# Cross-attention and mixture-of-experts layer: router logits from the first norm, a second list ahead, a new last expert, new slots

## The reference

```python
f   = layernorm(x)
h   = tanh(ctx @ Ws + f @ W + b)              # for every (token, context row)
rho = h @ w, masked;  att = softmax(rho)
t   = att @ ctx
x   = x + tanh(t . Wcw + bcw) * f + tanh(t . Wcb + bcb)   # two numbers per token
y   = layernorm(x)
probs = softmax(y @ gate)                     # 8 experts
# each expert takes the 512 tokens with its highest probabilities
out = x + gelu(y @ Ws1 + bs1) @ Ws2 + bs2
for e in experts: out[tokens_e] += probs * (gelu(y[tokens_e] @ W1[e] + b1[e]) @ W2[e] + b2[e])
```

## Time and profile before

| | |
|---|---|
| three executions | 950.3, 953.3, 953.63 us (median 953.3) |
| profiled execution, its own time | 951.22 us |
| its span, first to last instruction | 949.5 us |
| mean granted TensorE clock | 0.973 of full speed |
| busy TensorE, ScalarE, VectorE, GpSimd | 814.7, 768.4, 723.5, 200.5 us |
| DMA traffic | 41.84 MB |

### The profile page before, as it was taken

One profiled execution on the slowest core, in us unless ns is written; L12 is line 12 of the kernel. 1 busy time (PEld: TensorE's weight loads), 2 busy tenths in 40 slices (PEclk: granted clock), 3 DMA queues, 4 the chain that ended last, 5 costly groups with the idle time before them and its releaser, 6 DMA issues.

```text
span 949.5 us, 14380 instructions
## 1 busy us (share of the span) xinstructions
PE 814.7 (86%) x5519; PEld 477.7 (50%) x5519; DVE 723.5 (76%) x1482; ACT 768.4 (81%) x601; POOL 200.5 (21%) x434
## 2 busy tenths in 40 slices
PE   6855776668999988999988899987998799999993
PEld 4311221124454443545434454545877688898883
DVE  6898898989877789887698976958864667666530
ACT  4999999999999999999799979965624466766751
POOL 2110220050230041211006000220000154444522
PEclk9999999999999999999999899997999899999997
DMA  8000000010001002000000100013121335555422
GB/s 263 5 0 1 1 1 1 1 43 3 1 2 45 1 21 69 1 1 23 1 1 23 45 1 20 4 31 125 45 73 39 112 89 134 134 133 130 94 23 23
DMA packets 32408, 41.84 MB, mean 44 GB/s; under 512 B 2365, under 2 KB 29011, under 8 KB 32339
## 3 DMA queue, kind: packets, MB, share of 16 engines
q1 hardware_dynamic: 26083, 32.49, 10.4%
q0 software_dynamic: 6144, 8.39, 5.4%
q10 hardware_dynamic: 112, 0.04, 0.0%
HBM read 28.33 MB, written 12.58 MB: 43 GB/s over the span
## 4 chain that ended last, share of the span: by engine, by line
PE 52%; ACT 22%; DVE 16%; issue 6%; POOL 3%; DMA 0%; ACTq 0%; DVEq 0%; POOLq 0%
ACT z L916 18%; PE bank L725 12%; PE bank L850 9%; PE bank L873 9%; PE bank L783 8%; DVE z L1239 7%; PE bank L768 6%; PE bank L701 2%; ACT z L912 2%; PE bank L654 1%; DVE xn L1160 1%; POOL out_dram L1145 1%; ACT u L956 1%; DVE onehot L1527 1%; PE bank L779 1%
## 5 line engine op out<-in xcount | busy, mean ns | idle before, releaser
L916 ACT ACTIVATE z<-z 128x4096 f32<-128x4096 f32 (+5 forms) x157 | 510.3, 3289 | 7.4 <-DVE z L1239 7.3
L1239 DVE TENSOR_SCALAR z<-feat,txt_bias 128x1024 f32<-128x1024 f32 (+1 forms) x704 | 406.5, 649 | 24.9 <-PE bank L725 24.6
L725 PE MATMUL bank<-z,window 128*32 128x512 f32 x2464 | 309.3, 607 | 77.8 <-ACT z L916 75.7
L725 PEld LDWEIGHTS bank<-z,window 128*32 128x32 f32 x2464 | 69.4, 110 | 268.3 <-issue 136.4
L783 PE MATMUL bank<-ws_sb,u 128*128 128x256 f32 x512 | 130.5, 397 | 4.8 <-ACT u L956 4.8
L783 PEld LDWEIGHTS bank<-ws_sb,u 128*128 128x128 f32 x512 | 95.0, 194 | 43.6 <-issue 23.3
L768 PE MATMUL bank<-tr,ws_s 128*128 128x512 f32 x384 | 110.6, 424 | 0.0
L850 PE MATMUL bank<-xg_s,w_s 128*128 128x512 f32 x384 | 101.2, 400 | 3.4 <-DVE xg_s L1553 3.4
L1559 DVE TENSOR_TENSOR hid_s<-hid,hid_s 128x512 fp32r<-128x512 f32 x64 | 44.2, 691 | 76.5 <-ACT hid_s L996 76.5
L873 PE MATMUL bank<-w_s,hid_s 128*128 128x256 f32 x768 | 102.5, 283 | 0.0
L873 PEld LDWEIGHTS bank<-w_s,hid_s 128*128 128x128 f32 x768 | 99.6, 190 | 5.5
(11 more groups left out here) (227 smaller groups left out, 671.4 us busy)
## 6 DMA issues: line engine op xcount, KB each, us to landing
w_raw<-in_L_ffn_W_dram SPq DMA_DIRECT2D x16, 1024.0 KB, 5.5
x_ring<-in_x_dram SPq DMA_DIRECT2D x8, 512.0 KB, 8.1
xn_dram<-xn SPq DMA_DIRECT2D x8, 512.0 KB, 2.9
out_dram<-x_ring SPq DMA_DIRECT2D x8, 512.0 KB, 3.0
u<-in_L_ffn_Ws_dram SPq DMA_DIRECT2D x1, 1024.0 KB, 11.3
ws_sb<-in_L_ffn_Ws_dram SPq DMA_DIRECT2D x1, 1024.0 KB, 13.8
xg<-xn_dram,idx POOLq DMA_INDIRECT x32, 4.1
out_dram<-y,idx POOLq DMA_INDIRECT x32, 3.9
```

What stands on the lines that cost most here:

```text
L725: ins = e.matmul(sums[v][32 * r:32 * r + 32, :], window[:, c, 31 - k:63 - k], z[:, n % ZB, at_piece:at_piece + TOK], start=(v, r) not in b ...
L916: e.activation(part, part, ACT.Tanh).then_inc(signal(*step), 1)
L1239: ins = e.tensor_scalar(z[:, n % ZB, i * width:(i + 1) * width], feat_of(units, c), bias_of(units, t, c), None, ALU.add)
```

## The change

1. **Logits.** `logits` becomes a part of `pre`: TensorE multiplies the turned first norm `tr_x` (stationary, tokens as output rows) with the gate (8 columns), 8 matmuls per unit. `x_spread` (GpSimd) keeps the root of the variance; `logits_out` (VectorE) multiplies by it; `logits_shift` multiplies by the second scale and shifts by the maximum, right after `y_scale`. `gate_cols`, `lg_t` and `logits_turn` go.
2. **Slots.** New tables, `SPLITS` in place of `EARLY_PAIR` and `LATE_SPLIT`; the tail of unit 0 hangs on the end of unit 0, no longer on the start of the next batch; each unit's FFN has its own start and step, with `up` one slot earlier.
3. **Chain.** `router` of unit 6 moves forward; norm, turn and store of unit 7 stand behind `probs_out`; `y_hi` (ScalarE) makes the high part of its turn, `split_hi` of expert 0's weights goes into the tests.
4. **Lists.** List 1 is made before expert 0, with filler between; expert 0 has the beside-steps of every other expert. `EXPERT_FILL` may put filler into expert 0. Experts sum in the banks `RHO` (even) and `DOWN` (odd).
5. **Last expert.** All its ups come first; then token tile by token tile all downs (`e_tile`), `e_out`, and the tile's scatter. The high and low parts of its last four slices go to `last_s`, in the place of the first weights.

```diff
-EARLY_PAIR, LATE_SPLIT = 8, 8
+SPLITS = ((10, 20), (0, 20), (0, 20), (0, 7))
-PRE_EARLY = (20, 21, 22, 23, 24, 24, 25, 26, 26)
-PRE_LATE = (27, 28, 30, 31, 32, 32, 33, 34, 34)
-TAIL_EARLY = (-1, 0, 1, 3, 4, 5, 6, 7, 9, 9, 10, 11, 12, 11, 12, 13)
-TAIL_LATE = (-1, 1, 2, 3, 6, 7, 8, 9, 12, 14, 15, 16, 17, 16, 17, 18)
-TAIL_SINGLE = (-1, 0, 1, 2, 3, 4, 5, 6, 8, 8, 9, 10, 10, 10, 11, 11)
-FFN = (15, 2.2)
-FFN_LAST = (14, 1.7)
+PRE_FIRST = (0, 0, 1, 2, 2, 3, 3, 3, 4, 6, 6)
+PRE_EARLY = (20, 20, 21, 22, 22, 23, 25, 25, 27, 29, 30)
+PRE_LATE = (27, 28, 30, 31, 32, 32, 32, 34, 34, 35, 38)
+TAIL_EARLY = (-1, 0, 1, 3, 3, 4, 5, 8, 9, 10, 10, 11, 13, 13)
+TAIL_FIRST = (-1, 0, 1, 3, 3, 5, 6, 7, 9, 9, 9, 10, 12, 12)
+TAIL_LATE = (-1, 1, 2, 3, 6, 7, 9, 9, 12, 13, 16, 16, 18, 18)
+TAIL_SINGLE = (-1, 0, 1, 2, 3, 5, 6, 10, 8, 9, 9, 9, 12, 11)
+FFN_PLACES = (-1, 1, 2)
+FFN = ((12, 2.0), (33, 2.3), (14, 2.2), (36, 2.2), (14, 1.7), (26, 1.6))
-TAIL_FILL = (2, 4, 0, 0)
-READY_FILL = (1, 0)
-TEST_FILL = (1, 2, 2, 2, 3, 3, 2, 2, 2, 3)
-RANK_FILL = (0, 1, 2, 3)
-LIST_FILL = (2, 1, 0, 1)
+TAIL_FILL = (3, 0, 2)
+READY_FILL = (0, 1)
+TEST_FILL = (2, 3, 2, 3, 2, 1, 1, 2, 3, 1)
+RANK_FILL = (1, 1, 4, 1)
+EXPERT_FILL = (4, 0, 3)
+SECOND_FILL = (7, 5, 1)
+LIST_FILL = (2, 1, 0, 2)
...
-        at_slots(base, TAIL_EARLY, tail(early))
+        at_slots(ends_at[early] + 1, TAIL_EARLY if early else TAIL_FIRST, tail(early))
...
+    n = 0
+    for v, (begin, step) in enumerate(FFN):
+        for m in range(M):
+            n = max(n, starts[v // UPB + 1] + begin + int(step * m))
+            at_slots(n, FFN_PLACES, [[("up", v, m, 0, passes)], [("gelu", v, m)], [("down", v, m, 0, J)]])
+        at_slots(n, (FFN_PLACES[-1] + 1,), [down_ends(v)])
...
-    order += [*end[0], *end[1], ("load_w1", 0), ("load_w2", 0), *end[2], ("att_exp", vb), ("logits_exp", va)]
+    order += [*end[0], *end[1], ("load_w1", 0), ("load_w2", 0), *end[2], ("att_exp", vb), ("logits_exp", va), ("router", va)]
     fill_chain(TAIL_FILL[0])
-    order += [*end[4], *end[5], *end[6], *end[7]]
+    order += [*end[4], *end[5], *end[6], *held, ("exp_again",)]
+    held.clear()
     fill_chain(TAIL_FILL[1])
-    order += [("exp_again",), *end[8], *end[9], *first_split, *ended]
+    order += [*end[7], *end[8], *ended, ("logits_exp", vb), ("router", vb), ("values", NT - 2 * J, NT)]
     fill(TAIL_FILL[2])
-    order += [*end[10], *end[11], *end[13], ("router", va)]
-    fill(TAIL_FILL[3])
-    order += [*end[14], *end[15], ("logits_exp", vb), ("router", vb), ("values", NT - 2 * J, NT)]
+    order += held
     for hf in range(NH):
         order += [("probs_turn", hf), ("probs_out", hf)]
     order += [("load_w1", 1), ("load_w2", 1)]
+    order += [*end[9], *end[10]]
     fill(READY_FILL[0])
...
+    beside = [end[11], end[12], *beside]
+    by_scalar = [[("y_hi", vb, c) for c in range(C)], *[[step] for step in first_split]]
     for k in range(TESTS):
-        order += [("count", k), ("sign_count", k), ("total", k), *held]
+        order += [("count", k), ("sign_count", k), ("total", k), *held, *(by_scalar.pop(0) if by_scalar else [])]
         fill_test(TEST_FILL[k])
         order += [*([("low_digits",)] if k == 0 else beside.pop(0) if beside else []), ("decide", k), ("ask", k)]
...
-    order += [("listed", 0), ("fold", 0), ("folded", 0), ("gather", 0), ("mark", 1), ("mark_slots", 1, 0), ("mark_slots", 1, 1)]
+    order += [("listed", 0), ("fold", 0), ("folded", 0), ("gather", 0)]
+    fill(SECOND_FILL[0])
+    order += [("mark", 1), *(("mark_slots", 1, q) for q in range(4))]
+    fill(SECOND_FILL[1])
+    order += [*(("list", 1, q) for q in range(4)), ("listed", 1)]
+    fill(SECOND_FILL[2])
+    order += [("fold", 1), ("folded", 1), ("gather", 1)]
...
-        if ex == 0:
-            if m < 3:
-                steps += listing(1, *((2,), (3, "list"), ("fold",))[m])
-            elif m < 7:
-                steps += listing(2, *(("mark", 0), (1, 2), (3, "list"), ("fold",))[m - 3])
-        elif m < 6:
+        if m < 6:
             steps += listing(ex + 2, *(("mark",), (0,), (1,), (2, 3), ("list",), ("fold",))[m])
...
+    for m in range(LAG, M):
+        order += up(E - 1, m)
+    for a in range(A):
+        order += [("e_tile", a), ("e_out", E - 1, a)]
+    order.append(("scatter", E - 1))
...
                 elif kind == "logits":
                     v, = args
...
+                    e.wait_ge(*done("x_turned", v, 0))
+                    e.wait_ge(*done("x_turned" if v else "x_turned_first", v, C - 1))
+                    e.wait_ge(loaded["gate"], 16)
                     dst = take(MISC[0])
-                    for c in range(C):
-                        for i in (1, 0):
-                            for j in range(J):
-                                ins = e.matmul(dst[32 * j:32 * j + 32, 0:P], gate_cols[:, c, :],
-                                               tr[:, v % 2, i, c, j * P:(j + 1) * P].bitcast(F32),
-                                               start=c == 0 and i == 1, stop=c == C - 1 and i == 0)
+                    for j in range(J):
+                        for c in range(C):
+                            ins = e.matmul(dst[:, j * E:(j + 1) * E], tr_x[:, c, j * P:(j + 1) * P], gate_sb[:, c, :],
+                                           start=c == 0, stop=c == C - 1)
...
+                elif kind == "e_tile":
...
+                    e.matmul(part, b2_row[:, ex:ex + 1].broadcast_to([B2_ROWS, P]), b2_s[:], start=True, stop=False)
+                    for m in range(M):
+                        if a == 0:
+                            e.wait_ge(*done("e_lo", ex, m))
+                        for term, (i, j) in enumerate(SPLIT_TERMS):
+                            ins = e.matmul(part, slice_of(ex, m)[:, i, a * P:(a + 1) * P], w2_s[ex % 2][:, j, m, :],
+                                           start=False, stop=m == M - 1 and term == 2)
```

151 lines of the change are left out of this document (80 added, 71 removed).

## The result

The changed kernel takes 942.1 us (median of 4, 940.6 to 942.7) against 952.6 (950.3 to 953.6) for the kernel before: ratio 0.9891, 95% interval 0.9868 to 0.9914. It is faster by about 10 us, half of the 21 forecast, and 0.1 us outside the range. The profiled execution took 942.6 us (span 940.9).

The account below looks back on a forecast made before the run. ScalarE, TensorE and VectorE were near their limits in the tanh phase, TensorE full in experts 1 to 6. 951.2 - 3 - 4.9 + 2.0 - 10.1 - 5.2 = 930.0, adjusted to 931 us; range 922 to 942.

Parts of the forecast that it names:

- Tanh phase, -3: Tanh phase to the end of the last `rho`: new slots and logits save 3 us, bounds -14 and +7.
- TensorE gains about 1 us a unit: Tanh phase: new logits at 1.8 us a unit replace old ones at some 2.7, including the waiting before them.
- The price by the 7-column row: Tanh phase: 16 logits instructions priced like a 7-column row, two taking 0.22 us, so 1.8 us a unit.
- a quarter of the waits goes: Tanh phase: of ScalarE's 18.2 us of waits for `up` matmuls and VectorE's adds, 4.5 us go.
- Rival 1: Tanh phase: extra TensorE work in the last batch or VectorE's in the first becomes waits, +7, 941 us; chance 0.14.
- Chain, -4.9: Steps from the last `rho` to the tests: reordering and fewer steps save 4.9 us, bounds -6.5 and -3.
- 21 to 22 us after the last tanh: Expected profile sign behind the tanh phase: the first test starts 21 to 22 us after the last tanh.
- Tests to the first expert, +2.0: From the tests to expert 0: half `down` -0.9, turn +1.1, list and fold +0.8, store wait +1; bounds -1 and +7.
- Rival 4: Tests to first expert: TensorE stays at 1.2 GHz, 22 us of matmuls cost 22 us more, near 985 at worst; chance 0.04.
- Store, 1 of 0 to 1.7: Before `slots`: unit 7's store stands behind expert 1's weight loads, VectorE waits 0 to 1.7 us, taken as 1.
- First expert, -10.1: Expert 0: with list 1 and its gather ahead, TensorE's waits go, saving 10.1 us; bounds -10.6 and -4.
- Last expert, -5.2: Last expert: TensorE ends unchanged, three of four scatters go out under later tiles, saving 5.2 us; bounds -5.6 and -3.

Follow-up runs that it names:

- the nine profiles: Profiles of nine kernels that keep the changed kernel's tanh phase unedited; last `rho` ended from 637.6 to 646.5 us, on average at 641.7.
- both repairs: Changed kernel with the tests' FFN pieces placed as before the change and unit 7's store ahead of expert 1's weight loads: 0.9850, 940.1 us.

## Why the forecast was too low

The total was 11 us off. By steps:

1. **Tanh phase, -3: measured +0.4.** The sum was nearly right, its parts were not. "TensorE gains about 1 us a unit" failed: 15.6 us of busy time with 6.7 idle in front, 22.3 in all, is no less than the old 9.7 + 11.8 = 21.5. The price by the 7-column row (1.8 us a unit, measured 1.95) was good; the old waits were wrongly credited. And "a quarter of the waits goes" saw only the waits for `up`; as those went, VectorE's took their place (6.4 to 17.6). Half of the rise was in the first batch (5.8 us before 200 us, for 0.2), into which unit 0's tail and more single blocks had moved; undone alone, neither made the kernel faster, so which of them costs is open. Not in the forecast at all: `logits_shift` stands right behind `y_scale`, and VectorE waits for GpSimd there, 14.7 us in all seven units in which GpSimd scales (the kernel before waited 10.7 us at its norms). Rival 1 named this, at +7 instead of -3; the profile came a third of the way, and the average of the nine profiles (last `rho` at 641.7, +3.1 on the one profile before) would be six tenths.
2. **Chain, -4.9: measured -3.9.** Missed: the bias and half `down` that TensorE had to run between a late `down_end` and `probs`, at half clock; one piece less there gave 1.3 us. The sign "21 to 22 us after the last tanh" does not follow from the sum, which takes 4.9 us from 29.3; measured 25.9.
3. **Tests to the first expert, +2.0: measured +9.5. This is the step that failed.** The forecast counted what is added (a turn, a list) and took the early pieces as harmless, with 2 us of low clock only in its bound. Placed as before, they give 6.3 back (+3.2 is left); with the store moved too it is +2.2. Pieces stand in the first tests, where TensorE runs at 1.2 GHz (0.50 granted), and are missing in the middle. Windows of the changed kernel behind the first tests:

```profile
664.00:672.00 8.00, 8.00 (x42) 6.95 (x42) 5.94 (x31) 6.01 (x17) 0.00 (x0) 0.98 0.01 2
672.00:684.00 12.00, 8.95 (x44) 6.86 (x43) 10.85 (x52) 9.56 (x30) 0.00 (x0) 1.00 0.07 6
684.00:692.50 8.50, 8.07 (x34) 6.82 (x35) 6.80 (x34) 5.05 (x17) 0.00 (x0) 0.80 0.28 116
700.00:710.00 10.00, 10.00 (x40) 7.23 (x40) 7.41 (x12) 0.69 (x1) 0.00 (x0) 0.73 0.17 59
```

   TensorE is full in the first window and then idle for 3 of 12 us at the full clock. Behind that the clock falls again, twice (0.80, 0.73). How much of the cost is the clock and how much the pieces' order in TensorE's queue was not told apart. Rival 4 had the low clock and not its size: after 8 us the clock rose (0.98), as the Trainium skill has it ("TensorE: Matmul & The Clock Gate", What's actually happening), but it did not stay.
4. **Store, 1 of 0 to 1.7: measured 1.14.** The store behind the load landed 7.6 us after its issue at 693.75, the median is 2.9. The sum 693.34 + 5.5 + 2.9 = 701.7 is near its landing at 701.35, but not by its terms: the load took 6.7 us to land (5.3 in the kernel with the store ahead of it), and the store landed 1.3 us behind it. So the two overlapped in part. The Trainium skill ("DMA: Bandwidth & Descriptors", Queues, rings and completion order) has descriptors consumed in ring order on each DMA engine; the trace agrees in so far as the store landed last. Landings of the tile `xn_dram`, its eight stores and 32 gathers:

```profile
DMA to landing us min/median/max: 2.8/2.9/7.6
```

5. **First expert, -10.1: measured -10.6**, and undone alone +11.5.
6. **Last expert, -5.2: measured -4.2** (3.9 undone alone). The scatters went as forecast; the mis-sized term is TensorE's end, taken as unchanged: tile by tile it came 1.2 us later.

Step 3's 7.5 us of miss, taken off 942.1, would leave 934.6. The kernel with both repairs has step 3 as forecast and took 940.1: its last `rho` came 7.5 us later in its profile. So the failed step is shown in its stretch, and in the total some 2 to 4 us of it; the rest of the 11 us stands against a tanh phase whose end moves by 9 us from profile to profile, of which 3.9 us are one wait for GpSimd and the rest is open.

## What to carry to other kernels

Where a bottleneck engine's waits are named by one partner, look up how near the next partner is before counting them as gain: here 11.8 us of waits only changed their releaser. When filler work is moved, cost it at the clock granted in its new place and ask which instruction of the critical loop is queued behind it; taking one entry out of the chain moved 4 us. Where one phase ends anywhere in 9 us with the same code, judge an edit behind it by its stretch first, and by the total only with many executions. Price a replacement against the whole of what it replaces and test tables of slots together with the work that they were made for.
